# The last sums of a decoder layer: one batch of four added by GpSimd beside VectorE

## What is computed

```python
x = x + _L0_attn_ref(_layernorm(x), ...)             # gated Toeplitz mixer
x = x + _L0_xattn_ref(_layernorm(x), ctx_1024, ...)  # linear cross attention, 16 heads
x = x + _L0_ffn_ref(_layernorm(x), ...)              # 8 experts, the best 2 for each token
return x
```

```python
out = jnp.einsum('ned,ne->nd', y, combine)   # combine has 2 entries other than 0 for each token
x = x + out
```

## Time and profile before

| what | us |
|---|---|
| three runs | 280.78, 282.14, 282.83 |
| median of them | 282.14 |
| the profiled execution | 283.0 |
| its span, from the first to the last instruction | 281.2 |

### The profile page before, as it was taken

How to read it: one execution, slowest core, us unless ns; L and a number is a source line. 1 busy time by engine, 2 the same in 40 slices (tenths; PEclk the granted TensorE clock), 3 DMA queues, 4 the chain that set the end, 5 groups by cost and what they waited for, 6 DMA issues and landing times.

```text
span 281.2 us, 5724 instructions
## 1 busy us (share of the span) xinstructions
PE 248.3 (88%) x1697; PEld 211.8 (75%) x1697; DVE 190.4 (68%) x713; ACT 163.8 (58%) x343; POOL 124.2 (44%) x183
## 2 busy tenths in 40 slices
PE   7889999999999999989999999899699969999700
PEld 4647767686778999879987998777599969999600
DVE  3785759589658988998888888999866222232215
ACT  2556556564677777667767677653266645565400
POOL 5538999941101000227121722072337777776610
PEclk9999999999999999999999999999999999999965
DMA  6999999910004000001000100015888389993157
GB/s 208 288 235 200 215 196 203 204 26 0 2 1 149 2 0 3 1 0 59 19 3 0 58 21 1 2 47 157 232 228 243 127 252 303 309 253 105 40 181 267
DMA packets 38446, 34.05 MB, mean 121 GB/s; under 512 B 3581, under 2 KB 31234, under 8 KB 38288
## 3 DMA queue, kind: packets, MB, share of 16 engines
q1 hardware_dynamic: 35312, 28.96, 43.2%
q0 software_dynamic: 2272, 4.24, 4.3%
q10 hardware_dynamic: 832, 0.49, 0.6%
HBM read 19.80 MB, written 14.32 MB: 121 GB/s over the span
## 4 chain that ended last, share of the span: by engine, by line
PE 52%; DVE 25%; DMA 7%; POOL 7%; issue 5%; SPq 1%; ACT 1%; ACTq 0%; DVEq 0%; POOLq 0%
DVE X L918 11%; PE num L1180 10%; PE bank L1255 7%; PE bank L1141 5%; PE num L1119 5%; PE num L1265 3%; POOL expert_out L562 3%; PE bank L245 3%; PE num L245 3%; PE bank L1083 3%; PE num L247 2%; PE bank L247 2%; PE num L246 2%; PE bank L246 2%; DMA X<-in_x 2%
## 5 line engine op out<-in xcount | busy, mean ns | idle before, releaser
L918 DVE SCALAR_TENSOR_TENSOR X<-num,rden,X 128x128 f32<-128x128 f32 x256 | 72.1, 344 | 6.6
L1180 PEld LDWEIGHTS num<-kvw_sb,q 128*128 128x128 f32 x512 | 65.9, 190 | 12.1 <-ACT q L579 5.7
L1180 PE MATMUL num<-kvw_sb,q 128*128 128x130 f32 x512 | 68.7, 277 | 3.6 <-DVE X L918 3.6
L662 ACT ACTIVATE relu_z<-bank 128x512 f32<-128x512 f32 x64 | 38.1, 596 | 21.7 <-PE bank L247 21.6
L542 POOL DMA_INDIRECT dispatched<-rows,slot_i x32 | 31.3, 977 | 40.4 <-DVE rows L984 31.6
L562 POOL DMA_INDIRECT expert_out<-yo,xb x39 | 38.1, 977 | 18.1 <-issue 10.7
L579 ACT ACTIVATE q<-relu_z 128x512 f32<-128x512 f32 x64 | 40.4, 632 | 6.7 <-DVE acc L837 0.8
L1018 DVE TENSOR_TENSOR hid<-bank,silu_g 128x256 f32<-128x256 f32 x39 | 16.6, 424 | 38.5 <-ACT silu_g L687 38.2
L1255 PE MATMUL bank<-xT,wgu_sb 128*128 128x128 f32 x312 | 41.4, 276 | 0.3 <-ACT xT L579 0.3
L1255 PEld LDWEIGHTS bank<-xT,wgu_sb 128*128 128x128 f32 x312 | 38.0, 192 | 0.6 <-issue 0.6
L245 PE MATMUL bank<-y2T_hi,feat_hi 128*128 128x512 f32 x64 | 30.4, 476 | 0.2
(11 more groups left out here) (170 smaller groups left out, 402.8 us busy)
## 6 DMA issues: line engine op xcount, KB each, us to landing
wgu_sb<-in_wgu SPq DMA_DIRECT2D x39, 256.0 KB, 3.7
dispatched<-pad_row SPq DMA_DIRECT2D x3, 2795.0 KB, 33.1
xb<-dispatched SPq DMA_DIRECT2D x39, 65.0 KB, 3.3
y_back<-expert_out SPq DMA_DIRECT2D x4, 512.0 KB, 4.9
wd_sb<-in_wd SPq DMA_DIRECT2D x1, 1024.0 KB, 4.8
out<-X SPq DMA_DIRECT2D x4, 256.0 KB, 2.4
X<-in_x SPq DMA_DIRECT2D x3, 256.0 KB, 6.2
expert_out<-yo,xb POOLq DMA_INDIRECT x39, 3.7
```

The source lines that it names most:

```text
L662: a.activation(relu_z[:, k % 2, :], z_bank[k % 2], ACT.Relu).then_inc(relu_done, 1)
L918: v.scalar_tensor_tensor(tile_of(n, t), banks[:, t // 2, t % 2, 0:P], rden[:, h % 2, t:t + 1], tile_of(n, t), ALU.mult, ALU.add).then_inc( ...
L1180: nc.tensor.matmul(num[:, 2 * (h % 2) + t // 2, HA * (t % 2):HA * (t % 2 + 1)], q[:, h % 4, part], kvw_h, start=True, stop=True).then_inc( ...
```

## The change

The sums of the second batch (n = 1) move from DVE to POOL, with a semaphore of their own, `pool_add`. DVE does batches 0, 2, 3. SP stores in the order 0, 2, 1, 3. The loads and their order stay.

```diff
+        pool_add = sem("pool_add")
...
+        POOL_SUM, SUMS = 1, (0, 2, 3)
...
             for n in range(NB):
                 sp.dma_start(y_back[:, n, :, :].rearrange("p k c -> p (k c)"), ys_view[n, :, :]).then_inc(ld_y[n], 16)
-            for n in range(NB):
-                sp.wait_ge(add_step, 2 * (n + 1))
+            for n in (*SUMS[0:2], POOL_SUM, *SUMS[2:]):
+                if n == POOL_SUM:
+                    sp.wait_ge(pool_add, TOPK)
+                else:
+                    sp.wait_ge(add_step, TOPK * (SUMS.index(n) + 1))
                 sp.dma_start(out_view[n, :, :, :], X[:, TPB * n:TPB * (n + 1), :]).then_inc(stored, 16)
...
             pipeline(pool, [(2, send)], beside={5: [lambda t=t: scatter(NB - 1, t) for t in range(TPB)]})
+
+            pool.wait_ge(ld_y[POOL_SUM], 16)
+            pool.wait_ge(att_done, (POOL_SUM + 1) * H * TPB)
+            part = X[:, TPB * POOL_SUM:TPB * (POOL_SUM + 1), :].rearrange("p t c -> p (t c)")
+            for k in range(TOPK):
+                if k:
+                    pool.wait_ge(pool_add, k)
+                g.tensor_tensor(part, part, y_back[:, POOL_SUM, k, :], ALU.add).then_inc(pool_add, 1)
...
-            for n in range(NB):
+            for i, n in enumerate(SUMS):
                 dve.wait_ge(ld_y[n], 16)
                 part = X[:, TPB * n:TPB * (n + 1), :].rearrange("p t c -> p (t c)")
                 for k in range(TOPK):
                     v.tensor_tensor(part, part, y_back[:, n, k, :], ALU.add).then_inc(add_step, 1)
                     if k == 0:
-                        dve.wait_ge(add_step, 2 * n + 1)
+                        dve.wait_ge(add_step, TOPK * i + 1)
```

## The result

| | us |
|---|---|
| before, four runs | 280.78, 280.79, 282.14, 282.83; median 281.47 |
| with the change, four runs | 284.22, 284.94, 286.45, 286.81; median 285.69 |
| ratio | 1.0134, 95% interval 1.0096 to 1.0172 |
| profiled execution with the change, its span | 286.81, 285.0 |

The forecast was 283.1, within 281.4 to 284.7, and no measurable change. It came out 1.3% slower by the ratio, some 3.8 us, and above the range.

What follows compares the result with a forecast made beforehand. The last 12 us were taken as bound by the `y_back` loads, with VectorE's adds close behind. Colliding adds gave +0.94 us, other terms nothing; on the 282.14 median that made 283.1 us, range 281.4 to 284.7.

Steps and rivals of the forecast that it cites:

- The loads bound the gain: Tail: VectorE's adds hardly lag the loads of `y_back`, so no more than 0.2 us can come back.
- The two engines' adds exclude each other: Tail: VectorE and GpSimd adds reading SBUF block one another, moving the last add by +0.94 us.
- b1: GpSimd's second add of the second batch, forecast to run from 276.2 to 277.5; 1.28 us taken for its length.
- a2: VectorE's first add of the third batch, forecast to run from 275.60 to 276.29, almost unhindered.
- a3: VectorE's second add of the third batch, forecast to get on at 277.37 and end at 278.05.
- The reordering of the stores costs nothing there: SP's stores at the end: the new order was costed at nothing, the last store landing 2.3 us after issue.
- The drain: Rival at the end of GpSimd's queue: its 7.07 us drain begins after its second add; +3.8 us, 285.9; chance 0.07.

Runs made afterwards that it cites:

- e7: Kernel before, all sums on VectorE, but sums and stores in the order first, third, second, fourth: tail 15.1 us, no ratio.
- e6: As e2, but GpSimd starts its two adds only when VectorE's six are done: tail 17.9 us, no ratio.
- e9: As e2, but with the stores in the order of the batches: ratio 1.0019, tail 14.7 us.
- e2: The change with one more GpSimd drain between its last scatter and its two adds: ratio 1.0056, tail 15.3 us.
- e5: Kernel before, plus a GpSimd memset behind the last sum and a GpSimd drain ahead of the last batch's third norm: tail 15.4 us, no ratio.
- e4: Kernel before, but GpSimd waits for the last sum before its final drain, without added work: tail 17.6 us, no ratio.

## Why the prediction was wrong

**The loads bound the gain: right.** VectorE waits 1.14 us for the third load (e7 and the change alike), the adds of the last batch follow the fourth.

**The two engines' adds exclude each other: right, in size too.** +0.94 us were forecast for the last add, +0.9 came. The place also: b1 in the gap between a2 and a3. e6 shows the cause.

**"The reordering of the stores costs nothing there": wrong, 0.5 us.** The sum had the last three stores at 278.1, 278.5 and 279.4, so it knew how close they stand; measured, they are issued at 279.4, 279.9 and 280.8, with nearly the same gaps. But it kept the landing time of the earlier trace rows, 2.3 us, which came from stores 1.3 us apart. It was 2.8 us. e9, where the last store leaves 1.3 us behind the one ahead and lands after 2.3, shows the cause.

**The drain: the step that failed.** The 7 us of the earlier trace rows were seen and priced as a rival, at a chance of 0.07, with the argument that "the last work is an indirect write; the 7 us would be spent by then". The step that failed is this conclusion. The drain does belong to the scatters (e2, e5), but its time does not run off while the queue waits; it starts when the queue reaches the drain (e4). A wait placed ahead of it moves all of it behind the wait. The rival had the place right: b1 ended 10.3 us behind the last scatter's start, where the forecast had it (277.5), and the drain did pass the last store's landing. Its price was too high. It counted 7.07 us, of which 5.9 are the drain's own (the row begins before the last scatter has even started), and 0.4 for the barrier, where 0.2 were measured: some 1.3 us too much for the tail. That its span of 285.0 is the measured one to the digit is luck, since 1.4 us of the measured span lie ahead of the tail. Behind the later stores of the change, the drain costs 1.0 us.

In sum: adds 0.9, store 0.5, drain 1.0, together 2.4 us, of which the forecast had 0.94. With the missing 1.5 us the forecast would have been 284.6, still inside the range by 0.1; the measured median is 285.69. The runs of each kernel spread by 2.1 and 2.6 us, and what lies between the tail's 2.4 us and the ratio's 3.8 no run explains. The median of before moved too, from 282.14 on three runs to 281.47 on four, which put the forecast's base 0.7 us high and so worked the other way.

**What would beat both kernels?** None found. The best form of the change (e9) is within noise of before and its tail is 0.7 us longer. The first GpSimd add fell into the time in which VectorE waits for its load and cost nothing. The second met VectorE's a3 and held it up by 0.94 us. Against that, the two adds that VectorE is spared give back almost nothing, since it waits for its loads.

## What to carry to other kernels

Before adding anything to the end of an engine's queue, look at what the end of the program still waits for on that queue, drains included; a long drain that ends early is work that is hidden, and it is hidden only as long as the queue reaches it early. Where GpSimd has issued many indirect transfers and has an idle stretch, try an explicit drain there: in e2 it was over 0.2 us before the queue had work again and cost nothing. Adds moved from VectorE to GpSimd when both read two operands from SBUF take turns with VectorE's where they meet (a3 took 1.63 us in place of 0.69), and stores whose issues are pushed together land later (2.8 us in place of 2.3).

## What had not been expected of the hardware

- GpSimd's final drain took about 0.083 us for each indirect transfer since the drain before: 5.87 us for 71, 3.90 us for 47, and 0.07 us in e2, where none was left. A drain in the middle does not fit: 2.9 us for 24 (e5). It does not shorten while the queue waits: 5.9 us at once behind the last scatter and 5.87 us when 10 us later (e4). What it does in that time, no run shows.
- The profile's chain and waits did not show this drain. With 4.3 us of span behind the last add, the chain ended at the add, and the wait at the barrier was put down to another engine. It was found in the rows of L60.
- With all loads landed, a last store of 256 KB landed 2.3 us after its issue when the ones ahead were issued 1.3 and 1.9 us earlier (e9), and 2.8 us when they were issued 0.9 and 1.3 us earlier (e2), or with one 0.4 us ahead (e6).
